# Two PSUM banks for the token transposes, the selector made earlier, and one split of combine weights ahead of a softplus

## What is computed

```
xn = layernorm(x)
x  = x + attn0(xn) + ffn0(xn)
xn = layernorm(x)
x  = x + attn1(xn) + ffn1(xn)
```

## Time and profile before

| | us |
|---|---|
| median of three runs | 450.45 |
| lowest, highest | 447.9, 452.01 |
| the profiled execution, its own time | 449.16 |
| its span, from the first to the last instruction | 447.4 |

### The profile page before, as it was taken

The page is one execution under the profiler, slowest core; times in us unless marked ns, Lnnn a source line. Parts: engine busy times, 40 slices in busy tenths (PEclk is TensorE's granted clock), DMA queues, the critical chain, the costliest instruction groups (busy, mean ns, idle before and its releaser), DMA issues. The chain is left out here.

```text
span 447.4 us, 5697 instructions
## 1 busy us (share of the span) xinstructions
PE 342.4 (77%) x1491; PEld 243.4 (54%) x1491; DVE 349.4 (78%) x614; ACT 266.3 (60%) x461; POOL 224.0 (50%) x224
## 2 busy tenths in 40 slices
PE   0846779947798587888802679989797898989986
PEld 0536659736687576777701354546353465455452
DVE  5769999887996596958309797799998278998894
ACT  2478583464557647465432689786847347867830
POOL 3465600541675376778850893357833214455550
PEclk9996595867998899999965879999899599999989
DMA  6365100010111012911036000472447224767674
GB/s 174 89 192 142 37 0 2 24 35 7 36 51 40 24 45 54 181 37 37 25 114 186 0 0 0 95 140 50 93 96 141 47 47 96 141 143 146 135 141 94
DMA packets 34244, 35.08 MB, mean 78 GB/s; under 512 B 11734, under 2 KB 28359, under 8 KB 34215
## 3 DMA queue, kind: packets, MB, share of 16 engines
q0 software_dynamic: 7104, 21.90, 23.6%
q1 hardware_dynamic: 27110, 12.83, 10.7%
HBM read 13.29 MB, written 4.65 MB: 40 GB/s over the span
## 5 line engine op out<-in xcount | busy, mean ns | idle before, releaser
L585 POOL TENSOR_SCALAR state<-state,ssm_cb 128x1024 f32<-128x1024 f32 x32 | 38.2, 1194 | 78.4 <-DVE state L1268 78.1
L1268 DVE TENSOR_TENSOR_SCAN state<-dec,win_t 128x1024 f32<-128x1024 f32 x32 | 74.7, 2335 | 2.9 <-ACT dec L832 2.7
L517 POOL DMA_INDIRECT parts<-t_out,part x39 | 42.3, 1083 | 39.6 <-ACT t_out L739 31.5
L1619 PE MATMUL psum<-hid,g_w 128*128 128x512 f32 x128 | 60.7, 595 | 0.0
L505 POOL DMA_INDIRECT x_tile<-normed,token x39 | 41.6, 1068 | 13.4 <-issue 11.0
L730 ACT ACTIVATE t_hid_t<-psum 128x384 f32<-128x384 f32 x39 | 19.2, 492 | 37.6 <-PE psum L1482 37.6
L1153 DVE TENSOR_TENSOR t_hid<-t_sil,psum 128x352 f32<-128x352 f32 x39 | 20.3, 521 | 26.5 <-ACT t_sil L723 22.3
L299 PE MATMUL psum<-xn_hi,g_hi 128*128 128x512 f32 x64 | 36.4, 570 | 1.6 <-ACT at_all L801 1.4
L1493 PE MATMUL psum<-w_out,t_hid_t 128*128 x234 | 36.1, 292 | 1.3 <-ACT t_out L739 1.0
L1619 PEld LDWEIGHTS psum<-hid,g_w 128*128 128x128 f32 x128 | 24.5, 191 | 19.2 <-issue 17.0
L832 ACT ACTIVATE dec<-dt_t,ssm_a 128x1022 f32<-128x1022 f32 x32 | 34.1, 1136 | 0.1
(11 more groups left out here) (317 smaller groups left out, 934.5 us busy)
## 6 DMA issues: line engine op xcount, KB each, us to landing
xn_tok<-state POOLq DMA_DIRECT2D x16, 512.0 KB, 4.5
at_all<-state POOLq DMA_DIRECT2D x16, 512.0 KB, 4.4
e_raw<-in_L_ffn_w SPq DMA_DIRECT2D x16, 128.0 KB, 2.2
both<-parts SPq DMA_DIRECT2D x4, 512.0 KB, 5.4
e_raw<-in_L_ffn_w SPq DMA_DIRECT2D x8, 176.0 KB, 2.8
res<-in_L_attn_x SPq DMA_DIRECT2D x4, 256.0 KB, 3.8
normed<-rows SPq DMA_DIRECT2D x1, 1024.0 KB, 5.6
g_raw<-in_L_ffn_w SPq DMA_DIRECT2D x4, 256.0 KB, 5.1
```

The lines of the kernel that those rows point to most:

```text
L517: pool.indirect_dma_start(out=parts, out_offset=bass.IndirectOffsetOnAxis(ap=part[:, n:n + 1], axis=0), in_=t_out[n % ORING][:, :], in_off ...
L585: own(pool.tensor_scalar(state[k][:, :], state[k][:, :], ssm_cb[:, n:n + 1], 0.0, ALU.mult, ALU.add))
L1268: dve.tensor_tensor_scan(state[m % 4][:, :], dec[m % DECS][:, :], win_t[:, h * HTOK:(h + 1) * HTOK], 0.0, ALU.mult, ALU.add).then_inc(scan ...
L1619: pe.matmul(ps[4 + b][:, :], second, hid[v % HRING][:, :], start=what[0:2] == ("shared", 0) and b < NBLK - 1, stop=what[0:2] == ("expert", ...
```

## The change

It has three parts. First, the transposed tiles alternate between bank 4 and bank 7 (`X_BANKS`); at the steps of a `wo` product and the step after it they stay in bank 4, since bank 7 then holds that product. `turn_x(n)` waits for the split of the last tile in the same bank, which is mostly tile n - 2, and, once a `wo` product has used bank 7, for its `add`. `attention` gets a wait for the last tile that was in bank 7. Second, GpSimd's six selector instructions move from n = 31, 33, 35 to n = 12, 14, 16 (`sel_a`) and 20, 22, 24 (`sel_b`), one at each. Third, in turn (0, 3) `split_cw(2)` runs ahead of `softplus(2)`.

```diff
--- before.py
+++ after.py
@@ -355,6 +355,12 @@
         BK_DVE = counted([what for n in range(NTILE + 3) for what in beside(n, BACK_OPS)], BACK_OPS)
         BACK_ACT = {"sin": 3, "double": 2}
         BK_ACT = counted([what for n in range(NTILE + 3) for what in beside(n, BACK_ACT)], BACK_ACT)
+
+        WO_AT = [first + BACK_STEPS["wo"] for first in BACK_AT]
+        X_BANKS = [X_BANK]
+        for tile in range(1, NTILE):
+            other = X_BANK if X_BANKS[-1] == ATT_BANK else ATT_BANK
+            X_BANKS.append(X_BANK if tile - 2 in WO_AT or tile - 3 in WO_AT else other)
 
         HB, HT, HTOK = NBLK // 2, NT // 2, NTOK // 2
         TURNS, GPT = 4, NG // 4
@@ -518,6 +524,9 @@
                     out=parts, out_offset=bass.IndirectOffsetOnAxis(ap=part[:, n:n + 1], axis=0),
                     in_=t_out[n % ORING][:, :], in_offset=None).then_inc(o_sent[n % ORING], 16)
 
+            SELECTOR_AT = {12: (sel_a, 0, None), 14: (sel_a, 0, 0), 16: (sel_a, 0, E1), 20: (sel_b, SPLIT_A * GE, None),
+                           22: (sel_b, SPLIT_A * GE, 0), 24: (sel_b, SPLIT_A * GE, E1)}
+
             def prepare(n):
 
                 if n == 27:
@@ -527,16 +536,16 @@
                 if n == 29:
                     split(sw1_raw[:, :, :], sw1_hi[:, :, :], sw1_lo[:, :, :])
                     pool.nop().then_inc(weights_split, 1)
-                if n == 31:
-                    own(pool.memset(sel_a[:, :].bitcast(F32), 0.0))
-                    own(pool.memset(sel_b[:, :].bitcast(F32), 0.0))
-                if n in (33, 35):
-                    for part, first_e in ((sel_a, 0), (sel_b, SPLIT_A * GE)):
+                if n in SELECTOR_AT:
+                    part, first_e, at_e = SELECTOR_AT[n]
+                    if at_e is None:
+                        own(pool.memset(part[:, :].bitcast(F32), 0.0))
+                    else:
                         part = part[:, :].rearrange("p (c h) -> p c h", h=H1)
                         own(pool.affine_select(out=part, in_=part.bitcast(F32), compare_op=ALU.not_equal, fill=1.0,
-                                               base=-E1 * ((n - 33) // 2) - first_e, pattern=[[-1, part.shape[1]], [0, H1]],
+                                               base=-at_e - first_e, pattern=[[-1, part.shape[1]], [0, H1]],
                                                channel_multiplier=1))
-                if n == 35:
+                if n == max(SELECTOR_AT):
                     pool.nop().then_inc(sel_ready, 1)
 
             for n in range(NTILE):
@@ -713,7 +722,7 @@
                 act.wait_ge(x_turned, n + 1)
                 if n >= TRING:
                     act.wait_ge(h0_made, n - TRING + 1)
-                act.activation(xt_hi[n % TRING][:, :], ps[X_BANK][:, 0:P], ACT.Copy).then_inc(x_hi_ready, 1)
+                act.activation(xt_hi[n % TRING][:, :], ps[X_BANKS[n]][:, 0:P], ACT.Copy).then_inc(x_hi_ready, 1)
 
             def tile_silu(n):
 
@@ -1142,7 +1151,7 @@
             def split_x(n):
 
                 dve.wait_ge(x_hi_ready, n + 1)
-                dve.tensor_tensor(xt_lo[n % TRING][:, :], ps[X_BANK][:, 0:P], xt_hi[n % TRING][:, :].bitcast(F32),
+                dve.tensor_tensor(xt_lo[n % TRING][:, :], ps[X_BANKS[n]][:, 0:P], xt_hi[n % TRING][:, :].bitcast(F32),
                                   ALU.subtract).then_inc(x_lo_ready, 1)
 
             def gate(n):
@@ -1333,13 +1342,12 @@
                     combine(1)
                     poly(2)
                 if (h, i) == (0, 3):
+                    split_cw(2)
                     softplus(2)
                 for s in range(GSTEPS):
                     if s in ((2, 4, 6), (1, 2, 4))[(h, i) == TURN_LIST[-1]]:
                         scan(scans_next)
                         scans_next += 1
-                    if (h, i, s) == (0, 3, 2):
-                        split_cw(2)
                     if (h, i, s) == (0, 3, 3):
                         split_cw(3)
                     if (h, i, s) == (0, 3, 5):
@@ -1439,6 +1447,7 @@
 
             def attention(b):
                 pe.wait_ge(back_dve, BK_DVE["sum", b])
+                pe.wait_ge(x_lo_ready, max(t for t in range(min(NTILE, WO_AT[b] + 3)) if X_BANKS[t] == ATT_BANK) + 1)
                 for n in range(TPB):
                     ins = pe.matmul(ps[ATT_BANK][:, n * P:(n + 1) * P], held["kv"][b][:, n * P:(n + 1) * P],
                                     wo_sb[:, :], start=True, stop=True)
@@ -1450,9 +1459,13 @@
             def turn_x(n):
 
                 pe.wait_ge(x_tile_in[n % XRING], 16 * (n // XRING + 1))
-                if n >= 1:
-                    pe.wait_ge(x_lo_ready, n)
-                pe.transpose(ps[X_BANK][:, 0:P], x_tile[n % XRING][:, 0:D], ident[:, :]).then_inc(x_turned, 1)
+                bank = X_BANKS[n]
+                if bank in X_BANKS[:n]:
+                    pe.wait_ge(x_lo_ready, max(t for t in range(n) if X_BANKS[t] == bank) + 1)
+                done = [b for b, at_step in enumerate(WO_AT) if at_step < n - 2]
+                if bank == ATT_BANK and done:
+                    pe.wait_ge(back_dve, BK_DVE["add", done[-1]])
+                pe.transpose(ps[bank][:, 0:P], x_tile[n % XRING][:, 0:D], ident[:, :]).then_inc(x_turned, 1)
 
             def hidden(n):
 
```

## The result

The changed kernel takes 437.14 us (median of 4 runs, 436.63 to 439.03) against 449.55 of the kernel before (4 runs): a ratio of 0.9727, 95% interval 0.967 to 0.9784. The forecast was 436.5 within 432 to 443.5. The sum came out close, but two of its terms did not: the banks brought less and the split more than was worked out, and these two errors partly cancel.

A forecast was written before the change was run, and what follows sets the result against it. No engine was full in the tile loop; a chain through several engines paced it. Loop's end 3.6, banks 3.7 and split 6.0 gave 13.3 us, from 449.8 to 436.5, range 432 to 443.5.

The forecast's parts named there:

- The sum: Whole kernel: 3.6 + 3.7 + 6.0 = 13.3 us gained, from a start of 449.8 to 436.5 us.
- The loop's end (3.6): End of tile loop: without the selector there, the last scatter follows its `t_out` at 0.30 us, gaining 3.6 us.
- A stall shrinks by 1.03: Tile loop, from step 16: with two banks `hidden` starts 0.20 us after the gate instead of 1.23.
- The banks' gain up to tile 13 (3.1): Tile loop up to tile 13: three stalls count, at 1.03 us each, 3.1 us in all.
- The added waits, "I take 0": Waits for `add` in `turn_x` and the low part in `attention`: cost 0, the tile coming two steps after the product.
- The bound of 2.1: Upper cost of the new waits for `add`: three places of at most 0.7 us each, 2.1 us.
- The banks' gain at the end (3.7): Whole tile loop: two banks gain 3.7 us, taken between 3.1 and GpSimd's limit of 4.3; bounds 0 and 8.2.
- other five: Stalls after tile 13, where GpSimd is nearly full: up to 5.2 us more if all count.
- limits the whole gain to 4.3: Tile 38: GpSimd's full row lets its transpose move from 210.20 to 205.9 at best, 4.3 us.
- The rival "selects hold up VectorE": Tile loop: four selects hold VectorE up by 4 x 0.49 = 2.0 us, giving 438.5 us; chance 0.08.
- The rival "slower": Tile loop: longer TensorE idle pieces bring the low clock; twelve such steps lose 23 us, giving 459.7; chance 0.03.
- The split (6.0, bounds 4.2 to 6.5): Turn (0, 3): split ahead of softplus removes TensorE's 4.19 us wait and the low clock after it, 6.0 us.

The follow-up runs named there:

- e6_tail_bank: `e4_tail` with the tile four steps after a `wo` product also kept in bank 4, so no transpose stands behind `add`: 432.1 us, ratio 0.9587.
- e5_writes: The changed kernel with needless clears in the loop in place of the selector instructions, and the selector made behind the last scatter: 434.75 us, ratio 0.9652.
- e1_banks: The kernel before with only the two alternating banks and their waits; selector and split in their old places: 444.22 us, ratio 0.9874.
- e4_tail: The changed kernel with all six selector instructions moved behind the last scatter: 434.91 us, ratio 0.9665.
- e2_selector: The kernel before with only the selector instructions moved to their new, earlier places in the loop: 449.64 us, ratio 0.9993.
- e8_bank: The changed kernel, selects still in the loop, with the tile four steps after a `wo` product also kept in bank 4: 437.45 us, ratio 0.9743.
- e9_sw_tail: `e6_tail_bank` with the split of the shared weights (tile 29) also moved behind the last scatter, ahead of the selector: 434.48 us, ratio 0.966.

## Why the prediction was right, and where it was not

- **The loop's end (3.6).** Right: 3.87 us of lateness became 0.28, 3.6 gained, as worked out from the earlier trace rows.
- **A stall shrinks by 1.03.** Right within 0.05: from the gate's end to `hidden` 1.23 us became 0.25.
- **The banks' gain up to tile 13 (3.1).** Close: 3.72 in the changed kernel, 3.38 alone. The places were nearly those counted: 0.9 at the loop's start and 1.0 at tile 2 (the two first stalls, counted as one), 2.0 at tile 11 (step 14), 1.0 at tile 13 (step 16). That 1.0 was lost at tile 8 makes the fit of the sum in part luck.
- **The added waits, "I take 0".** Wrong. The reason given was that the tile in question is transposed two steps after the product; so it is (product in step 9, tile 13 in step 11), but its transpose still stands behind `add` (0.14 us after its end at the first place, a wait of 2.25 us at the second). The table shows it at tile 8, and `e6_tail_bank` gains 1.2 us at the last `t_out` and 2.8 in the median without that wait. The bound of 2.1 was nearer to it.
- **The banks' gain at the end (3.7).** This is the step that failed: 1.5 in the changed kernel. Alone they gave 4.26, but what I priced as GpSimd's time was VectorE's. The scatter of tile 13 at 151.16 and gather 38 at 203.01 lie near the marks worked out (152.46 and 203.3), in part by luck, since the loop began 1.12 us early: from scatter 13 to gather 38 GpSimd took 51.85 us and not 50.86. Its row was indeed full. But `e5_writes`, as full, loses 0.9 us, and the selects 3.0. The "other five" stalls that come later were miscounted, too: of the eight waits in the earlier trace rows six stand up to step 16 (92.58 to 150.33), and only two later:

```profile
175.08 0.30 PE L1455 MATMUL psum<-ident,x_tile 128*128 128x128 f32 x1 [1.16 <-DVE xt_lo L1145]
...
201.71 0.30 PE L1455 MATMUL psum<-ident,x_tile 128*128 128x128 f32 x1 [1.05 <-DVE xt_lo L1145]
```

  These two gave 0.8 to 1.0 us each (from tile 20 to 21 and from 29 to 30), in `e1_banks`, in `e6_tail_bank` and also after the change, with GpSimd's row full. So GpSimd's full row took nothing from these two; that a full row limits the whole gain to 4.3 was not tested. In `e6_tail_bank`, where neither the selects nor the wait for `add` take from it, the banks give 5.70.
- **The rival "selects hold up VectorE".** Right in its mechanism, at a chance of 0.08. Its price was 4 x 0.49; the one instruction in the earlier trace rows from which 0.49 was taken overlapped only part of GpSimd's split. With full overlap it is the whole select, 1.7 to 2.0 us each. The first select of `sel_a` made a wait of 1.7 us longer on TensorE, and the low clock behind the idle time cost another 1.7 (`e4_tail` against the changed kernel); that second half is in no price of the rival. The rival "slower" named the low clock in the loop, at a chance of 0.03, since the loop's waits were expected to get shorter.
- **The split (6.0, bounds 4.2 to 6.5).** Mechanism right, size too small: 7.2. The wait of 4.19 went as said. The rest, 1.9 by the sum, was 7.49 - 4.61 = 2.9. What stands from the first shared product to the weighing came as worked out (4.47 to 343.91 - 340.88 = 3.03; 3.1 forecast, though it counted two triples where three stand ahead of the `select`). What the sum left out is the second biases, which shrink with the clock too, from 2.07 to 1.12 us; the upper bound had them at 0.4 less:

```profile
349.80 2.07 PE L1607 MATMUL psum<-cw_b,b_sb 64*128 64x512 f32 x2
```

  The softplus behind it is shorter than before too: its masked copy takes 0.73 us and not 1.53; it now runs after the multiplication of GpSimd's `add_state` and not beside it, which is the likely cause, not a shown one.
- **The sum.** 13.3 forecast, 12.4 measured (449.55 - 437.14): 2.2 too much in the banks, 1.2 too little in the split; that the total comes within 1 us is luck to the extent that the two have opposite signs. In the profiled execution the earlier start (1.1) and a slower stretch between the layers (-1.1) cancel; the latter stretch varies by as much between kernels that have the same code there (111.66 after the change, 109.95 in `e2_selector`, 110.51 in `e8_bank`).

The Trainium skill, page "SBUF — State Buffer", section "Who interferes with whom", says that a VectorE instruction with two inputs in SBUF contends with a GpSimd instruction that reads SBUF and not with one that only writes. The runs agree on both halves: 0.69 became 2.42 beside a select and stayed 0.69 beside a clear. By that rule taken at full length (four selects, 2 x 1.83 + 2 x 0.72, an estimate from the earlier trace rows) up to 5.1 us would have been the price, and the forecast 436.5 + 5.1 = 441.6; measured were 3.0 (4.6 in `e2_selector`), and the selects of `sel_b` hardly lengthened VectorE's work; one was itself held (below).

Not settled: how the 0.9 us at the end of `e5_writes` divide between GpSimd's time, the wait for `add` with its low clock, and chance.

## What to carry to other kernels

Work for an engine that is "off the path" is not free because its queue has room: look at what runs beside it on VectorE, and put GpSimd instructions that read SBUF where VectorE waits for a transfer, as behind the last scatter here, and not so many that they reach into the work behind that wait (`e9_sw_tail`). A wait that gets a second buffer is worth what the work behind it starts earlier (1 us of 4.5 here), and each new wait that the second buffer brings has to be looked up at its place. Before a wait on TensorE is priced, read the granted clock behind it: here 4.2 us of waiting had 2.8 us of low clock in its wake.

## What was not expected of the hardware

- In `e2_selector` a VectorE instruction that had begun 0.14 to 0.21 us before GpSimd's select was held for the select's whole length (2.58 and 3.05 us for 0.68 and 1.21), and the select kept its 1.83 us. But it can also be GpSimd that is held: of the two selects of `sel_b` in the changed kernel, one takes 1.63 us instead of the 0.72 of the earlier trace rows, beside a scan that had begun 0.12 us before it and kept its time (1.64 in `e2_selector`, beside the same kind of scan, and 1.62 in `e8_bank`, where the scan beside it took 1.78 instead of 1.21):

```profile
181.50 1.25 DVE L1140 TENSOR_TENSOR_SCAN at_all<-at_all,turn_k 128x512 f32<-128x512 f32 x1
...
181.62 1.63 POOL L545 TENSOR_SCALAR_AFFINE_SELECT sel_b<-sel_b 128x512 fp32r<-128x512 f32 x1
```

  What decides which of the two is held stays open.
- A one-input `tensor_scalar` on VectorE beside a GpSimd clear took 0.97 us instead of 0.43, while the two-input instruction ahead of it, beside the same clear, was not slowed.
